# Clamp and reciprocal of an attention kernel's softmax correction moved from GpSimd to VectorE, and a head's copy placed one half step earlier

## The reference

```python
h = layernorm(x) * (1 + ca) + sa
q, k, v = h @ Wq, h @ Wk, h @ Wv            # per head: 16, 16 and 64 wide
sim = einsum('bnhk,bmhk->bnhm', q, k)
attn = softmax(sim / 4, axis=1)             # over the queries n, for each key m
o = einsum('bnhm,bmhv->bnhv', attn, v)
x = x + ga * (o @ Wo)
h = layernorm(x) * (1 + cb) + sb
x = x + gb * fp4_ffn(h)                     # gate, up, silu, down; blocks of 16 rounded to FP4
```

## Time and profile before

| | |
|---|---|
| median of three runs | 1725.67 us |
| the profiled execution's own time | 1725.48 us |
| its span | 1724.1 us |
| PE busy | 1650.4 us, 96% |
| DVE busy | 1590.5 us, 92% |
| ACT busy | 1362.6 us, 79% |
| POOL busy | 621.8 us, 36% |
| granted clock of TensorE, mean | 0.998 |

### The profile page before, as it was taken

The page is one execution under the profiler, slowest core; times in us unless marked ns, Lnnn a source line. Parts: engine busy times, 40 slices in busy tenths (PEclk is TensorE's granted clock), DMA queues, the critical chain, the costliest instruction groups (busy, mean ns, idle before and its releaser), DMA issues.

```text
span 1724.1 us, 37798 instructions
## 1 busy us (share of the span) xinstructions
PE 1650.4 (96%) x15114; PEld 813.0 (47%) x15114; DVE 1590.5 (92%) x1726; ACT 1362.6 (79%) x2488; POOL 621.8 (36%) x1339
## 2 busy tenths in 40 slices
PE   7999999999999999989999999999999999999997
PEld 6643333333333333763333332333333389999997
DVE  7889999999999999779999999999999678888886
ACT  5389999999999999559999999999999633333332
POOL 3023333333333333003633333333333365544442
PEclk9999999999999999999999999999999999999999
DMA  6102111111111112401111111111110422222200
GB/s 229 62 4 64 38 46 32 32 33 39 39 41 39 33 32 62 131 34 48 40 32 32 37 39 38 44 32 32 34 39 22 135 77 74 74 74 75 76 13 19
DMA packets 53018, 89.54 MB, mean 52 GB/s; under 512 B 3298, under 2 KB 34922, under 8 KB 52842
## 3 DMA queue, kind: packets, MB, share of 16 engines
q1 hardware_dynamic: 52426, 86.59, 15.4%
q10 hardware_dynamic: 416, 0.53, 0.1%
HBM read 57.74 MB, written 29.37 MB: 51 GB/s over the span
## 4 chain that ended last, share of the span: by engine, by line
DVE 66%; PE 28%; ACT 3%; issue 2%; POOL 1%; DMA 0%; DVEq 0%; ACTq 0%; POOLq 0%
DVE nm L1037 61%; PE slot L421 9%; PE acc L421 6%; PE acc L604 5%; PE acc L582 4%; ACT e_sb L776 2%; PE slot L638 1%; DVE ost L1050 1%; PE slot L553 1%; DVE v_sb L998 1%; PE slot L604 1%; PE slot L437 0%; PE acc L615 0%; DVE qs L1104 0%; DVE ost L942 0%
## 5 line engine op out<-in xcount | busy, mean ns | idle before, releaser
L1037 DVE TENSOR_REDUCE nm<-slot 128x1 f32<-128x1024 f32 x1024 | 1165.3, 1215 | 15.7 <-PE slot L553 15.7
L776 ACT ACTIVATE e_sb<-slot,nm 128x1024 f32<-128x1024 f32 x1024 | 1136.8, 1113 | 30.9 <-DVE nm L1037 28.7
L582 PE MATMUL acc<-e_sb,vp 64*64 64x512 f32 x8192 | 1066.0, 593 | 40.9 <-DVE ost L1050 38.6
L553 PE MATMUL slot<-stq,stk 64*64 64x512 f16 x4096 | 412.3, 388 | 0.0
L553 PEld LDWEIGHTS slot<-stq,stk 64*64 64x64 f16 x4096 | 118.5, 103 | 616.1 <-ACT e_sb L776 562.3
L582 PEld LDWEIGHTS acc<-e_sb,vp 64*64 64x64 f32 x8192 | 282.8, 132 | 207.3 <-issue 97.5
L1253 POOL TENSOR_TENSOR dlt<-nm 128x4 f32<-128x4 f32 x128 | 25.4, 198 | 605.2 <-DVE nm L1037 605.2
L776 ACT ACTIVATION_READ_ACCUMULATOR e_sb<-slot,nm 128x1 f32 x1024 | 200.1, 195 | 0.0
L1244 POOL TENSOR_TENSOR vp<-v_sb,fac 128x512 f32<-128x512 f32 x128 | 133.4, 1042 | 10.1 <-POOL fac L1234 0.2
L1230 POOL TENSOR_TENSOR rtot<-tot,mone 128x4 f32<-128x4 f32 x128 | 131.9, 1031 | 10.0
L1224 POOL TENSOR_TENSOR wsum<-cor,ssum 128x8 f32<-128x8 f32 x128 | 25.8, 202 | 228.5 <-ACT cor L804 228.5
(11 more groups left out here) (168 smaller groups left out, 1759.2 us busy)
## 6 DMA issues: line engine op xcount, KB each, us to landing
stk<-qk_parts SPq DMA_DIRECT2D x128, 128.0 KB
o_heads<-ost SPq DMA_DIRECT2D x64, 256.0 KB, 3.4
v_sb<-o_heads SPq DMA_DIRECT2D x8, 2048.0 KB, 8.2
v_sb<-in_x SPq DMA_DIRECT2D x16, 512.0 KB, 7.3
qk_parts<-e_sb SPq DMA_DIRECT2D x32, 256.0 KB, 2.2
stq<-qk_parts SPq DMA_DIRECT2D x128, 64.0 KB
out<-e_sb SPq DMA_DIRECT2D x32, 128.0 KB, 1.7
v_sb<-in_wgu SPq DMA_DIRECT2D x1, 1408.0 KB, 14.3
```

Source lines behind the costliest of these rows:

```text
L553: mm = pe.matmul(slot[s][side * VD:(side + 1) * VD, c * 512:(c + 1) * 512], stk[c * 64:c * 64 + 64, h % 2, i * P + side * VD:i * P + (side ...
L582: mm = pe.matmul(acc[half * VD:(half + 1) * VD, c * 512:(c + 1) * 512], vp[rows, g % 3, gi, half, :], e_v[rows, j % ERING, n0:n0 + 512], s ...
L776: act.activation(e_v[:, j % ERING, half * 1024:(half + 1) * 1024], slot[u % 3][:, :], ACT.Exp, bias=nm[:, g % 4, i, half:half + 1], accum_ ...
L1037: dve.tensor_reduce(nm[:, g % 4, i, half:half + 1], slot[u % 3][:, :], AX.X, ALU.max, negate=True).then_inc(maxed.sem)
```

## The change

The attention's correction is divided anew, with the same results to be made:

- The cut at zero of `dlt` goes from POOL to DVE. In DVE's order it stands behind the maximum of the first half of the step after the group. It waits for a new count, `diff_made`, that now means that the differences are there, and ACT waits for `diff_cut`.
- The power of -1 on POOL (L1230) becomes a reciprocal on DVE, behind the maximum of the first half of the second step after the group. It waits for `tot_made`, and POOL waits for `rtot_made` before it makes `fac`. POOL's `fac` and `vp` go one step later in its program.
- DVE's copy of `acc` at a head's end stands between the two halves of its step instead of behind them.
- The tile of minus ones is dropped.

```diff
@@ scalar engine, attend_act
-                        act.wait_ge(*diff_made.past(b * JG + g))
+                        act.wait_ge(*diff_cut.past(b * JG + g))
@@ vector engine, attend_dve
                 for half in range(2):
+                    if half == 1 and jv >= 0 and jv % NT == NT - 1:
+                        h = jv // NT
+                        dve.wait_ge(*attended.past(b * JT + jv))
+                        if b * H + h >= 2:
+                            dve.wait_ge(*o_out[h % 2].past((b * H + h - 2) // 2))
+                        dve.tensor_copy(ost[:, h % 2, 0:512], acc[:, 0:512]).then_inc(took_low.sem)
                     if j < JT:
                         maximum(b, j, half)
-                if jv >= 0 and jv % NT == NT - 1:
-                    h = jv // NT
-                    dve.wait_ge(*attended.past(b * JT + jv))
-                    if b * H + h >= 2:
-                        dve.wait_ge(*o_out[h % 2].past((b * H + h - 2) // 2))
-                    dve.tensor_copy(ost[:, h % 2, 0:512], acc[:, 0:512]).then_inc(took_low.sem)
+                    if half == 0 and j % GROUP == 0 and GROUP <= j <= JT:
+                        g = j // GROUP - 1
+                        dve.wait_ge(*diff_made.past(b * JG + g))
+                        dve.tensor_scalar(dlt[:, g % 4], dlt[:, g % 4], 0.0, None, ALU.min).then_inc(diff_cut.sem)
+                    if half == 0 and j % GROUP == 1 and GROUP <= j < JT + GROUP:
+                        g = j // GROUP - 1
+                        dve.wait_ge(*tot_made.past(b * JG + g))
+                        dve.reciprocal(rtot[:, g % 4, :], tot[:, g % 4, :]).then_inc(rtot_made.sem)
@@ GpSimd, attend_pool
-                    sem, n = pool_own.next()
-                    pool.tensor_tensor(tot[:, s, :], wsum[:, s, :, 0], wsum[:, s, :, 1], ALU.add).then_inc(sem)
-                    pool.wait_ge(sem, n)
-                    sem, n = pool_own.next()
-                    pool.tensor_tensor(rtot[:, s, :], tot[:, s, :], mone[:, :], ALU.pow).then_inc(sem)
-                    pool.wait_ge(sem, n)
+                    pool.tensor_tensor(tot[:, s, :], wsum[:, s, :, 0], wsum[:, s, :, 1], ALU.add).then_inc(tot_made.sem)
+                if j % GROUP == 1 and GROUP <= j < JT + GROUP:
                     h, i0 = divmod(GROUP * g, NT)
+                    pool.wait_ge(*rtot_made.past(b * JG + g))
...
-                    sem, n = pool_own.next()
-                    pool.tensor_tensor(dlt[:, s, :, 1], nm[:, s, :, 0], nm[:, s, :, 1], ALU.subtract).then_inc(sem)
-                    pool.wait_ge(sem, n)
-                    pool.tensor_scalar(dlt[:, s], dlt[:, s], 0.0, None, ALU.min).then_inc(diff_made.sem)
+                    pool.tensor_tensor(dlt[:, s, :, 1], nm[:, s, :, 0], nm[:, s, :, 1], ALU.subtract).then_inc(diff_made.sem)
```

More of the change, by code:

```diff
@@ L139, in adaln_block @@
         rtot = sb("rtot", [P, 4, GROUP])
-        mone = sb("mone", [P, GROUP])
         fac = sb("fac", [P, 4, GROUP, 2])
@@ L249, in adaln_block @@
         made_ident, made_half, rstd_made, wv_low = tally("made_ident"), tally("made_half"), tally("rstd_made"), tally("wv_low")
-        diff_made, vp_made = tally("diff_made"), tally("vp_made")
+        diff_made, tot_made, vp_made = tally("diff_made"), tally("tot_made"), tally("vp_made")
         wsq_made, root_made = tally("wsq_made"), tally("root_made")
@@ L265, in adaln_block @@
         rows_read, rows_made, gu_quant, dn_quant = tally("rows_read"), tally("rows_made"), tally("gu_quant"), tally("dn_quant")
-        maxed, took_low = tally("maxed"), tally("took_low")
+        maxed, diff_cut, rtot_made, took_low = tally("maxed"), tally("diff_cut"), tally("rtot_made"), tally("took_low")
         wgu_low, wdb_low, x2_made, moments = tally("wgu_low"), tally("wdb_low"), tally("x2_made"), tally("moments")
@@ L1311, in gpsimd_program @@
             pool.memset(quarter4[:, :, :], -0.25)
-            pool.memset(mone[:, :], -1.0)
             pool.memset(epsilon, EPS)
```

## The result

The changed kernel takes 1745.53 us in the median (1742.92 to 1745.73), the kernel before 1725.62 in the same comparison: a ratio of 1.0112, with a 95% interval of 1.0094 to 1.0130. It is slower by 19.9 us. I had predicted 1749.0, within 1740 to 1762.

The account below looks back on a forecast made before the run. DVE was taken to set the pace. Small instructions 22.3 us, batch passage 0.5 and lock 0.5 made 23.3 on the profiled 1725.5, 1748.8; with 0.2 for the median, 1749.0 us, range 1740 to 1762 (8 in 10).

Parts of the forecast that it names:

- The bound: Steady attention groups: DVE sets the pace, one maximum every 1.131 us, eight filling the group's 9.05 us.
- My sign that the maxima keep over 60% of the chain: Profile after the change: DVE's maxima should still have over 60% of the chain, against 61% before.
- The cut: Cut at zero on DVE, 128x8, 124 times on the path: 0.08 us each, by distance of starts.
- The reciprocal: Reciprocal on DVE, 128x4, once a group: 0.10 us each, by distance to the next start.
- my lower bound: Both small DVE instructions, if a maximum hid part of them: 0.07 us each, 17.4 us in all.
- The waits: Inputs from POOL in steady groups: ready 0.6 us early for the cut, 0.3 for the reciprocal; no waiting.
- The moved copy: DVE at a head's end: idle 0.34 us goes, a 0.48 wait before the copy comes; 0 +- 0.1, 30 times.
- Between the batches: The last group's reciprocal stands ahead of DVE's statistics; normalising starts at about 690.7 instead of 690.16: +0.5 us.
- The lock: POOL folding a weight holds DVE's cut in four groups, +0.2 us each, perhaps the reciprocal too: +0.5 to +1.
- B: Small DVE instructions cost their full durations, 0.35 us a group: 43.4 us instead of 22.3, total 1770; chance 0.13.
- C: A ring through scores, maximum and exponential sets the pace: 1715 us, or 1725.7 without the idle-time gain; chance 0.08.
- A: DVE reaches the reciprocal before its input: 0.2 us a group, 1774 us; chance 0.15, including POOL holding every cut.

## Why the prediction was right

*The bound.* DVE sets the pace of the attention: right, and shown from both sides by the added instructions, 0.48 us a head in either kernel. My sign that the maxima keep over 60% of the chain was wrong. I should have seen that a chain breaks off at idle time, and that the move leaves DVE none but the one that PE ends.

*The cut*, 0.08 predicted, 0.073 measured alone. *The reciprocal*, 0.10 predicted, 0.062 alone. This is the term that I mis-sized. The row that I took it from shows only the distance to the next start, and here too that is 0.09; but the maxima behind the reciprocal make up 0.03 of it. Why they do, no run shows. Both together came to 0.135 a group, 16.7 us instead of 22.3. The 0.07 each of my lower bound stood in no row, and it was nearly the measured mean; the bound of 17.4 was 0.7 too high.

The estimate of 16 us from the Trainium skill's page "Perfetto Trace Analysis", section "Optimizing Scalar/DVE Operations", was nearer than my rows. I had weighed one row of 0.10 against it.

*The waits* of the two small instructions: none, as predicted. The margins were 0.35 for the reciprocal (0.3 predicted) and 0.61 for the cut (0.6 predicted).

*The moved copy*: 0 +- 0.1 predicted at an end, +0.05 measured alone. The wait before it was 0.40 alone, as my sign said, 0.31 in the changed kernel, where the reciprocal stands ahead of it, and 0.23 where an unused instruction stands there as well: each takes up 0.08 to 0.09 of the wait. That also makes the whole, 0.54 a head, less than the sum of the parts, 0.59. PE waits 38.6 us at the 30 ends, now for ACT's copy, as foreseen.

*Between the batches*: +0.5 predicted, +0.4 measured. *The lock*: +0.5 predicted, none seen in the changed kernel. There a piece of POOL's ends just as the cut comes:

```profile
859.36 0.16 DVE L1053 TENSOR_SCALAR dlt<-dlt 128x8 f32<-128x8 f32 x1
```

```profile
858.69 0.73 POOL L1204 TENSOR_TENSOR wo_s<-wo_s,ga 128x256 f32<-128x256 f32 x1
```

The cut starts 0.06 before the piece ends, and its 0.16 is the usual length. The mechanism exists (0.5 us a time in both kernels with the unused instructions), but the cut all but misses it. The reciprocal, for which I had allowed as much again, is not held at all: all four that fall into these steps lie wholly inside a piece of POOL's and last 0.17.

*Not in the prediction at all*: the two spells of TensorE's lower clock, 1.5 us each, which the profile of the kernel before does not have; its four executions in that comparison lie within 0.4 us of each other. In four of five executions of the changed kernel the mean clock is 0.996 and the time is 1745.5 to 1745.7; in the fifth it is 0.997 and 1742.92. So my total of 23.3 consisted of 5.6 too much for the small instructions, 0.6 too much for the lock and the passage, and 3 missing for the clock. That 1749.0 lies so near 1745.53 is therefore luck. That the range held is not: without the 3 us the changed kernel would take about 1742.5, still within 1740 to 1762.

*The rivals.* B (the durations count, 0.35 a group) and C (a ring hides the additions) are refuted by the cut and the reciprocal alone and by the unused instructions. A was real as a mechanism and did not occur.

## What to carry to other kernels

Where one engine issues without a pause, read the price of an addition from the distance of starts on that engine, over several instructions behind it and not the next one alone; the work taken off an engine that had idle time brought nothing here. A chain of waits names one path: a single short wait a head turned most of the 61% from one engine to two others while the bound stayed. Unused work added to the engine showed that it did. A copy moved forward only swapped one wait for another here, because what held the other engine did not move; 0.24 us a head were won by giving the waiting engine its next independent work first.

## What the runs showed that I had not expected

The same idle of 2.58 us on TensorE was followed by the full clock in the kernel before and by 1.2 GHz in the changed one, whose instructions there are the same and 8.9 us later. The kernel before seems to have such executions too: in one comparison nine of its fifteen took 1725.1 to 1726.3 us with a mean clock of 0.998; the other six took 1727.1 to 1728.0, five of them with 0.996. Of the profiles of the eight experiments, three have both spells, three have one and two have none. What decides whether the clock falls I did not try, and it stays open. For reading, it means that a difference of 1.5 or 3 us between two versions of this kernel is not evidence on the edit, and the length of a head is.
